# Linear attention's scan: key-value products kept in their PSUM bank for the state scans, with the first product terms placed later in the order

## The chip, the cores and the metric

The kernel runs on one NeuronCore of a Trainium2 chip, as one program. The metric is the device time of one execution, in microseconds, lower is better. Engine names in the text: PE is TensorE, DVE is VectorE, ACT is ScalarE, POOL is GpSimd.

## What is computed

The whole program is a two-layer model on x of shape 16 x 256 x 128, all float32: a linear attention block with decaying state, a mixture of experts with capacity limits, a retention block, and two layers of windowed local attention with a feed-forward part. The change lies in the first of them. Cut to what matters:

```
q, k, v = x @ Wq.T, x @ Wk.T, x @ Wv.T          # 32 heads of D = 4
q, k = rope(q), rope(k); phi = elu(.) + 1
beta = clip(sigmoid(x @ Wbeta.T + b), 0.85, 0.9995)      # M = 2 decays a head
mix = softmax(x @ Wmix.T + b)
K = K * beta + phi_k                              # (D) for each m
S = S * beta + outer(phi_k, v)                    # (D x D) for each m
num = phi_q . S ;  den = phi_q . K + 1e-6
y = sum over m of num / den * mix
z = LN(x + y @ Wout.T + bout) * g + b ;  x = x + z
```

## The kernel before, in words

Activations lie transposed, 128 features on partitions and the 4096 tokens along the free dimension, cut into 8 chunks of 512 tokens (two sequences each). `linear_attention` handles one chunk in one step c of an unrolled loop that each engine writes out in its own order; engines meet only through counting semaphores. A step works on chunk c (states and sums), on chunk c+1 (its projections, rotation and features, called "more" in the code) and on chunk c-1 (its two layer norms, called "last").

A float32 matmul over 512 tokens is two passes on PE, shown in the profile as a pair. The eight PSUM banks are fixed: 0 and 1 take projections (k, q and their swapped forms) and the centred x, 2 is shared by denominators, values, variances and the router, 3 to 6 are the "spread" banks (BV + d), 7 collects the output sum.

For each of the four d (rows of the state) of a chunk:

- `keys_spread` (L494, PE) copies feature d of phi_k to all four rows of its head, into bank 3 + d.
- `outer` (L722, DVE) multiplies that bank with the values vs and writes `U[d]` in SBUF; this counts `u_done`.
- `state` (L726, DVE), twice for each d (states i = 2d and 2d + 1, one for each decay m), scans `S[i] = beta * S + U[d]` along the tokens. It counts `s_scan`.
- `queries_spread(c, i)` (L512, PE), i = 0 to 7, spreads the query share of decay i % 2 into bank 3 + i % 4. The first four of them take over a bank that keys_spread had filled, the other four a bank that an earlier term has read.
- `term(c, i)` (L734, DVE) multiplies that bank with S[i] into a buffer T[i % 4]; `summed(c, i)` (L519, PE) multiplies it with the output matrix and adds it up in bank 7.

Around these stand `rotate` (L699, L700, DVE), which empties banks 0 and 1, `rope` (L843), `key_dot` (L831), `divide` (L838) and `weigh` (L847) on POOL, `inverse` on ACT, `queries` (L482, L483, PE), and the norms of chunk c-1: `residual` (L738), `z_variance` (L529), `z_scale` (L742), `x_add` (L747), `x_centre` (L537), `router` (L546), `x_variance` (L562), `root` on ACT and `x_scale` (L758), the last DVE instruction of a step.

The guard that decides when the first four query spreads may overwrite their bank, and the scan:

```
                    if i < 4:
                        pe.wait_ge(u_done, 4 * c + i + 1)
                    else:
                        pe.wait_ge(t_done, NS * c + i - 3)
...
                    nc.vector.tensor_tensor(U[d][:], ps[BV + d][:], vs[c % 2][:], ALU.mult).then_inc(u_done, 1)
...
                    nc.vector.tensor_tensor_scan(S[i][:], beta[i % 2][:, chunk(c)], U[i // 2][:], 0.0,
```

Of the kernel before, what the change touches and what calls it, by code (L numbers as in the profile page):

```python
# [11 lines left out]
ALU = mybir.AluOpType  # L12
# [13 lines left out]
NH0, D0, M0 = 32, 4, 2  # L26
# [32 lines left out]
def chunk(c):  # L59
    return bass.ds(c * CH, CH)  # L60
# [282 lines left out]
def linear_attention(k, w):  # L343
    nc, ps = k.nc, k.ps
    with ExitStack() as big:
# [82 lines left out]
        with ExitStack() as ctx:  # L428
            buf = lambda n: k.sb(n, [P, CH], ctx=ctx)
            ka, kb, qa, qb, ek, eq, phk, phq = map(buf, ("ka", "kb", "qa", "qb", "ek", "eq", "phk", "phq"))  # L430
            vs = [buf(f"vs{i}") for i in range(2)]
            U = [buf(f"U{d}") for d in range(D0)]
            S = [buf(f"S{i}") for i in range(2 * D0)]
            K = [buf(f"K{m}") for m in range(M0)]
            mixed = [buf(f"phq_mixed{m}") for m in range(M0)]
# [32 lines left out]
            def _(pe):  # L468
# [37 lines left out]
                def queries_spread(c, i):  # L506
                    pe.wait_ge(shared, 2 * c + i % 2 + 1)
                    if i < 4:
                        pe.wait_ge(u_done, 4 * c + i + 1)
                    else:  # L510
                        pe.wait_ge(t_done, NS * c + i - 3)
                    nc.tensor.matmul(ps[BV + i % 4][:], w["spread"][:, i // 2, :], share[i % 2][:],  # L512
                                     start=True, stop=True).then_inc(p_mm, 1)

                def summed(c, i):
                    pe.wait_ge(t_done, NS * c + i + 1)
                    if i == 0 and c > 0:
                        pe.wait_ge(z_done, c)
                    nc.tensor.matmul(ps[BO][:], wout[:], TT[i % 4][:], start=(i == 0), stop=(i == NS - 1)).then_inc(sum_mm, 1)  # L519
# [44 lines left out]
                for c in range(-1, NCH + 1):  # L564
                    last, now, more = 0 < c, 0 <= c < NCH, c + 1 < NCH
                    if more:
                        keys(c + 1)
                    if last:
                        summed(c - 1, 6)
                        summed(c - 1, 7)  # L570
                    if now:
                        keys_spread(c, 2)
                        denominator(c, 0)
                    if more:
                        keys_swapped(c + 1)
                    if now:
                        denominator(c, 1)
                        keys_spread(c, 3)
                    if more:
                        values(c + 1)  # L580
                    if now:
                        queries_spread(c, 0)
                        queries_spread(c, 1)
                    if last:
                        z_variance(c - 1)
                    if more:
                        queries(c + 1)
                    if now:
                        queries_spread(c, 2)
                        queries_spread(c, 3)  # L590
                        summed(c, 0)
                        summed(c, 1)
                        queries_spread(c, 4)
                        queries_spread(c, 5)
                        summed(c, 2)
                        summed(c, 3)
                    if last:
                        x_centre(c - 1)
                    if now:
                        queries_spread(c, 6)  # L600
                        queries_spread(c, 7)
                    if 1 < c and c - 2 < EARLY // 4:
                        router(c - 2)
                    if last:
                        x_variance(c - 1)
                    if now:
                        summed(c, 4)
                        summed(c, 5)
                    if more:
                        keys_spread(c + 1, 0)  # L610
                        keys_spread(c + 1, 1)
# [80 lines left out]
            def _(dve):  # L692
# [3 lines left out]
                def rotate(c, which):  # L696
                    mm, a, b = ((k_mm, ka, kb), (q_mm, qa, qb))[which]
                    dve.wait_ge(mm, c + 1)
                    nc.vector.tensor_tensor(a[:], ps[BK][:], cos, ALU.mult)  # L699
                    nc.vector.tensor_tensor(b[:], ps[BKS][:], sin, ALU.mult).then_inc(rot, 1)  # L700

                def features(c, which):
                    e, x1, out = ((ek, kb, phk), (eq, qb, phq))[which]
                    dve.wait_ge(exped, 2 * c + 1 + which)
                    dve.wait_ge(plus1, 2 * c + 1 + which)
                    if c > 0 and which == 0:
                        dve.wait_ge(u_mm, 4 * c)
                    if c > 0 and which == 1:
                        dve.wait_ge(kp_done, 2 * c)
                        dve.wait_ge(mixed_r, 2 * c)  # L710
                    nc.vector.scalar_tensor_tensor(out[:], e[:], 1.0, x1[:], ALU.min, ALU.max).then_inc(phi, 1)
# [7 lines left out]
                def outer(c, d):  # L719
                    dve.wait_ge(u_mm, 4 * c + d + 1)  # L720
                    dve.wait_ge(v_sb, c + 1)
                    nc.vector.tensor_tensor(U[d][:], ps[BV + d][:], vs[c % 2][:], ALU.mult).then_inc(u_done, 1)  # L722

                def state(c, i):
                    dve.wait_ge(u_done, 4 * c + i // 2 + 1)
                    nc.vector.tensor_tensor_scan(S[i][:], beta[i % 2][:, chunk(c)], U[i // 2][:], 0.0,  # L726
                                                 ALU.mult, ALU.add).then_inc(s_scan, 1)

                def term(c, i):
                    dve.wait_ge(p_mm, NS * c + i + 1)  # L730
                    dve.wait_ge(s_scan, NS * c + i + 1)
                    if NS * c + i >= 4:
                        dve.wait_ge(sum_mm, NS * c + i - 3)
                    nc.vector.tensor_tensor(TT[i % 4][:], ps[BV + i % 4][:], S[i][:], ALU.mult).then_inc(t_done, 1)  # L734
# [25 lines left out]
                for c in range(-1, NCH + 1):  # L760
# [23 lines left out]
                    if now:  # L784
                        outer(c, 2)
                        state(c, 3)
                        term(c, 0)
                        term(c, 1)
                        outer(c, 3)
                        state(c, 4)  # L790
                    if more:
                        rotate(c + 1, 1)
                        features(c + 1, 0)
                    if now:
                        state(c, 5)
                        term(c, 2)
                    if last:
                        z_scale(c - 1)
                    if now:
                        term(c, 3)  # L800
                    if last:
                        x_add(c - 1)
                    if now:
                        state(c, 6)
                        term(c, 4)
                        term(c, 5)
                        state(c, 7)
                        term(c, 6)
                    if more:
                        features(c + 1, 1)  # L810
# [1721 lines left out]
```

## Time and profile before

| what | us |
|---|---|
| median of 3 runs | 1468.37 |
| lowest, highest run | 1466.29, 1468.88 |
| span of the profiled execution | 1407.0 |
| PE busy over the span | 1211.5 (86%) |
| DVE busy | 1044.5 (74%) |
| ACT busy | 884.2 (63%) |
| POOL busy | 841.7 (60%) |
| scan stage of linear attention, about 64 to 329 | 265 |

The profiled execution has no separate time of its own; its span runs from its first to its last instruction, and what lies outside that span is the difference to the runs, 1468.37 - 1407.0 = 61.4 us. Shares over the whole span are averages over stages with different limits, and the change touches one stage only, the stretch from 64 to about 304 us in which the chunks run through, so the views that count are those cut to one step of that stretch. A row of the timeline begins with the start in us from the span's start and the time the row covers; xN is how many instructions were merged in it, and the bracket is the idle time of that engine before it with what ended it.

### The profile page before, as it was taken

The numbers are of one execution on the slowest core, as the hardware profiler recorded it, in microseconds if no ns is written. First come the engines' busy times: TensorE is split into PE (matmuls) and PEld (weight loads), VectorE is DVE, ScalarE is ACT, GpSimd is POOL, SyncE is SP. The second block draws the span as 40 slices with busy tenths as digits, with TensorE's granted clock in tenths as the row PEclk, the third lists the DMA queues.
The fourth block names the chain that finished last, engine by engine and source line by source line (L and its number), as shares of the span: only waits on it lengthen the run. The fifth ranks groups of instructions, "written<-read, shape, count | busy, mean of one in ns | idle before, by whom it ended". The sixth has DMA issues, their size and how long they took to land. (4 is left out here: it accounts for less than half of the span.)

```text
span 1407.0 us, 26525 instructions
## 1 busy us (share of the span) xinstructions
PE 1211.5 (86%) x7852; PEld 790.4 (56%) x7852; DVE 1044.5 (74%) x2575; ACT 884.2 (63%) x2302; POOL 841.7 (60%) x774
## 2 busy tenths in 40 slices
PE   6879999973777999399689999998978999999797
PEld 3333344422556888234367777774656777777465
DVE  1289999885797998456488888874648888888564
ACT  6623333332444665067489989996648898899674
POOL 0045443514771666331788888886658887788663
PEclk9899999985898999589799999999999999999999
DMA  4800000001321221410000000000000000000001
GB/s 111 288 1 0 1 0 1 1 0 58 106 93 65 71 73 56 161 35 0 23 1 3 2 0 1 0 2 1 1 23 2 2 3 1 1 0 1 1 1 60
DMA packets 35021, 43.99 MB, mean 31 GB/s; under 512 B 5620, under 2 KB 24977, under 8 KB 34912
## 3 DMA queue, kind: packets, MB, share of 16 engines
q1 hardware_dynamic: 30304, 34.27, 7.5%
q0 software_dynamic: 4608, 8.47, 1.9%
q8 instruction: 43, 0.70, 0.2%
q14 instruction: 66, 0.54, 0.1%
HBM read 22.65 MB, written 21.12 MB: 31 GB/s over the span
## 5 line engine op out<-in xcount | busy, mean ns | idle before, releaser
L2099 DVE TENSOR_TENSOR R<-bank,tab 128x1024 f32<-128x1024 f32 x128 | 156.0, 1224 | 70.2 <-ACT sq L2009 69.4
L2043 ACT ACTIVATE W<-W,nm 128x128 f32<-128x128 f32 x512 | 198.3, 393 | 0.4
L1797 POOL TENSOR_TENSOR R<-R 128x512 f32<-128x512 f32 x128 | 161.1, 1280 | 16.0 <-DVE R L2099 16.0
L2122 DVE CUSTOM_DVE_ANT_0 W<-bank,mask_q,rn 128x128 f32<-128x128 f32 x512 | 147.5, 345 | 17.4 <-PE bank L1918 12.8
L1812 POOL TENSOR_TENSOR W<-W,rden 128x512 f32<-128x512 f32 x128 | 132.5, 1040 | 40.6 <-DVE rden L2129 35.2
L1308 POOL DMA_INDIRECT expert_rows<-Yt,xin x80 | 82.6, 1032 | 67.8 <-DVE Yt L1281 49.8
L1011 POOL DMA_INDIRECT expert_slots<-tok_rows,dst x64 | 67.5, 1054 | 66.4 <-ACT tok_rows L1035 45.6
L2043 ACT ACTIVATION_READ_ACCUMULATOR W<-W,nm 128x1 f32 x512 | 98.7, 193 | 0.0
L2027 ACT ACTIVATE QK<-bank 128x512 f32<-128x512 f32 x128 | 75.1, 587 | 35.6 <-PE bank L1893 33.7
L726 DVE TENSOR_TENSOR_SCAN S<-beta,U 128x512 f32<-128x512 f32 x64 | 93.5, 1483 | 0.0
L1943 PE MATMUL bank<-PT,VA 128*64 128x128 f32 (+1 forms) x1024 | 85.8, 261 | 3.7 <-ACT PT L2051 2.8
L1918 PE MATMUL bank<-QK 64*64 64x128 f32 x2048 | 86.1, 283 | 3.3 <-DVE nm L2122 3.0
L1806 POOL TENSOR_TENSOR R<-R,rn 128x512 f32<-128x512 f32 x64 | 66.7, 1042 | 31.3 <-ACT rn L2017 27.2
L2009 ACT ACTIVATE sq<-bank 128x512 f32<-128x512 f32 x128 | 74.6, 583 | 11.2 <-PE bank L1872 10.6
L2051 ACT ACTIVATE PT<-bank 128x512 f32<-128x512 f32 x128 | 74.9, 590 | 6.6 <-PE bank L1928 6.6
L2221 POOL TENSOR_TENSOR Uf_lo<-Uf,Uf_hi 128x512 fp32r<-128x512 f32 (+1 forms) x48 | 61.1, 1285 | 26.9 <-DVE Uf_hi L2378 26.2
L2106 DVE TENSOR_REDUCE sums<-sq 128x16 f32<-128x1024 f32 x64 | 76.9, 1201 | 0.0
L1928 PE MATMUL bank<-ident,W 128*128 128x128 f32 x512 | 75.6, 273 | 0.0
L1943 PEld LDWEIGHTS bank<-PT,VA 128*64 128x64 f32 x1024 | 52.0, 137 | 40.6 <-issue 40.5
L1872 PE MATMUL bank<-wqkv_hi,hs_hi 128*128 128x512 f32 x128 | 64.1, 501 | 10.5 <-ACT QK L2027 4.0
L1928 PEld LDWEIGHTS bank<-ident,W 128*128 128x128 f32 x512 | 62.5, 140 | 15.9 <-issue 0.7
L1918 PEld LDWEIGHTS bank<-QK 64*64 64x64 f32 x2048 | 55.3, 133 | 20.9 <-issue 16.9
(350 smaller groups left out, 3481.2 us busy)
## 6 DMA issues: line engine op xcount, KB each, us to landing
expert_slots<-empty SPq DMA_DIRECT2D x8, 650.0 KB, 6.6
xin<-expert_slots SPq DMA_DIRECT2D x8, 650.0 KB, 4.0
expert_rows<-empty SPq DMA_DIRECT2D x8, 512.0 KB, 6.7
pair_rows<-expert_rows SPq DMA_DIRECT2D x16, 256.0 KB, 4.4
expert_raw<-w1e_dram SPq DMA_DIRECT2D x9, 256.0 KB, 2.9
expert_raw<-w2e_dram SPq DMA_DIRECT2D x9, 256.0 KB, 3.2
tok<-x_dram SPq DMA_DIRECT2D x8, 256.0 KB, 4.7
out_dram<-tok_out SPq DMA_DIRECT2D x8, 256.0 KB, 2.6
```

The source lines that it names most:

```text
L726: nc.vector.tensor_tensor_scan(S[i][:], beta[i % 2][:, chunk(c)], U[i // 2][:], 0.0, ALU.mult, ALU.add).then_inc(s_scan, 1)
L1308: nc.gpsimd.indirect_dma_start(k.ys[:, :], bass.IndirectOffsetOnAxis(ap=ids, axis=0), Yt[:, s % 3, t, :], None, bounds_check=2 * T - 1, oo ...
L1797: nc.gpsimd.tensor_tensor(halves[:, :, 0, :, z, :], halves[:, :, 0, :, z, :], halves[:, :, 1, :, 1 - z, :], ALU.add).then_inc(summed, 1)
L1812: nc.gpsimd.tensor_tensor(x, x, scale.to_broadcast([P, 4, P]), ALU.mult).then_inc(scaled, 1)
L1918: m = nc.tensor.matmul(ps[BS[i]][r:r + WIN, blk // 2 * P:(blk // 2 + 1) * P], QK[par][rows, b, o:o + WIN], keys, start=True, stop=True)
L1928: m = nc.tensor.transpose(ps[BT[p % 2]][:, a * P:(a + 1) * P], W[:, p % RING, a * P:(a + 1) * P], k.const["ident"][:])
L1943: m = nc.tensor.matmul(ps[BO[p % 2]][i * DH:(i + 1) * DH, cols], v[:, 2 * b + i, :], PT[:, p % 2, i * SEQ + cols.start:i * SEQ + cols.stop ...
L2027: nc.scalar.activation(QK[par][:, qk * NB:(qk + 1) * NB, t * P:(t + 1) * P], ps[BX[(t + 1) % 2]][:].rearrange("p (a b) -> p a b", a=NB), A ...
L2043: m = nc.scalar.activation(x, x, ACT.Exp, scale=-1.0, bias=nm[:, p % RING, j:j + 1], accum_out=den[:, p % RING, j:j + 1])
L2099: nc.vector.tensor_tensor(R[:, i, qk, :, :].rearrange("p c (h d) -> p c h d", d=DH), x, y.to_broadcast([P, 2, HEADS, DH]), ALU.mult).then_ ...
L2106: nc.vector.tensor_reduce(sums[:, i, :, 0:1].rearrange("p h o -> p (h o)"), sq[:].rearrange("p q (h d) -> p (q h) d", d=DH), AX.X, ALU.add ...
L2122: m = nc.vector.tensor_tensor_reduce(W[:, p % RING, j * P:(j + 1) * P], ps[BS[i]][:, cols], k.const["mask_q"][:, cols], rn[:, par, 2 * s + ...
```

## The change

It drops the four buffers U. `outer` writes its product over the same bank that it reads, and the two scans of that d read the bank. As the bank is now needed until both scans are done, the first four `queries_spread` wait for the scans. On DVE the first terms are moved behind later scans: all eight scans are issued before term 3. On PE the sums of the terms are moved to match.

```diff
-            U = [buf(f"U{d}") for d in range(D0)]
@@ queries_spread
                     if i < 4:
-                        pe.wait_ge(u_done, 4 * c + i + 1)
+                        pe.wait_ge(s_scan, NS * c + 2 * i + 2)
@@ TensorE's order
                     if now:
+                        summed(c, 0)
                         queries_spread(c, 2)
+                        summed(c, 1)
                         queries_spread(c, 3)
-                        summed(c, 0)
-                        summed(c, 1)
+                        summed(c, 2)
                         queries_spread(c, 4)
                         queries_spread(c, 5)
-                        summed(c, 2)
-                        summed(c, 3)
                     if last:
                         x_centre(c - 1)
                     if now:
                         queries_spread(c, 6)
+                        summed(c, 3)
                         queries_spread(c, 7)
@@ outer, state
-                    nc.vector.tensor_tensor(U[d][:], ps[BV + d][:], vs[c % 2][:], ALU.mult).then_inc(u_done, 1)
+                    nc.vector.tensor_tensor(ps[BV + d][:], ps[BV + d][:], vs[c % 2][:], ALU.mult).then_inc(u_done, 1)
-                    nc.vector.tensor_tensor_scan(S[i][:], beta[i % 2][:, chunk(c)], U[i // 2][:], 0.0,
+                    nc.vector.tensor_tensor_scan(S[i][:], beta[i % 2][:, chunk(c)], ps[BV + i // 2][:], 0.0,
@@ VectorE's order
                         outer(c, 2)
                         state(c, 3)
-                        term(c, 0)
-                        term(c, 1)
                         outer(c, 3)
                         state(c, 4)
                     if more:
                         rotate(c + 1, 1)
+                    if now:
+                        term(c, 0)
+                        state(c, 5)
+                    if more:
                         features(c + 1, 0)
                     if now:
-                        state(c, 5)
-                        term(c, 2)
+                        term(c, 1)
+                        state(c, 6)
                     if last:
                         z_scale(c - 1)
                     if now:
-                        term(c, 3)
+                        term(c, 2)
+                        state(c, 7)
                     if last:
                         x_add(c - 1)
                     if now:
-                        state(c, 6)
+                        term(c, 3)
                         term(c, 4)
                         term(c, 5)
-                        state(c, 7)
                         term(c, 6)
```

TensorE, a middle chunk, from the second query spread to the sixth. Before (share0 and share1 are the query shares of the two decays, T0 to T3 the term buffers, z0_sq the square of the previous chunk's z):

```order
L512 MATMUL bank4<-phq_share1,spread 128x512 [waits u_done,phq_shared]
L529 MATMUL bank2<-z0_sq,mean 128x512 [waits v_sb,z_squared]
L482 MATMUL bank0<-H,wq0 128x512 [waits rot]
L483 MATMUL bank1<-H,wq0s 128x512
L512 MATMUL bank5<-phq_share0,spread 128x512 [waits u_done,phq_shared]
L512 MATMUL bank6<-phq_share1,spread 128x512 [waits u_done,phq_shared]
L519 MATMUL bank7<-T0,wout_centred 128x512 [waits z_done,t_done]
L519 MATMUL bank7<-T1,wout_centred 128x512 [waits t_done]
L512 MATMUL bank3<-phq_share0,spread 128x512 [waits t_done,phq_shared]
L512 MATMUL bank4<-phq_share1,spread 128x512 [waits t_done,phq_shared]
```

and in the changed kernel:

```order
L511 MATMUL bank4<-phq_share1,spread 128x512 [waits s_scan,phq_shared]
L528 MATMUL bank2<-z0_sq,mean 128x512 [waits v_sb,z_squared]
L481 MATMUL bank0<-H,wq0 128x512 [waits rot]
L482 MATMUL bank1<-H,wq0s 128x512
L518 MATMUL bank7<-T0,wout_centred 128x512 [waits z_done,t_done]
L511 MATMUL bank5<-phq_share0,spread 128x512 [waits s_scan,phq_shared]
L518 MATMUL bank7<-T1,wout_centred 128x512 [waits t_done]
L511 MATMUL bank6<-phq_share1,spread 128x512 [waits s_scan,phq_shared]
L518 MATMUL bank7<-T2,wout_centred 128x512 [waits t_done]
L511 MATMUL bank3<-phq_share0,spread 128x512 [waits t_done,phq_shared]
L511 MATMUL bank4<-phq_share1,spread 128x512 [waits t_done,phq_shared]
```

The spreads into banks 4, 5 and 6 now wait for scans instead of outer products, and the sums of T0 and T1 stand ahead of the spreads into banks 5 and 6.

VectorE, a middle chunk, the end of a step from the seventh state (S6) on. Before:

```order
L726 SCALAR_TENSOR_TENSOR S6<-beta0,U3 128x512 [waits u_done]
L734 TENSOR_TENSOR T0<-bank3,S4 128x512 [waits sum_mm,s_scan,p_mm]
L734 TENSOR_TENSOR T1<-bank4,S5 128x512 [waits sum_mm,s_scan,p_mm]
L726 SCALAR_TENSOR_TENSOR S7<-beta1,U3 128x512 [waits u_done]
L734 TENSOR_TENSOR T2<-bank5,S6 128x512 [waits sum_mm,s_scan,p_mm]
L711 SCALAR_TENSOR_TENSOR phq<-eq,qb 128x512 [waits kp_done,phq_mixed,plus1,exped]
L734 TENSOR_TENSOR T3<-bank6,S7 128x512 [waits sum_mm,s_scan,p_mm]
```

and in the changed kernel:

```order
L725 SCALAR_TENSOR_TENSOR S6<-beta0,bank6 128x512 [waits u_done]
L741 SCALAR_TENSOR_TENSOR zg0<-z0,vec0,z0_rs 128x512 [waits z_rstd]
L733 TENSOR_TENSOR T2<-bank5,S2 128x512 [waits sum_mm,s_scan,p_mm]
L725 SCALAR_TENSOR_TENSOR S7<-beta1,bank6 128x512 [waits u_done]
L746 TENSOR_TENSOR XT<-XT,zg0 128x512 [waits x_biased,z_scaled]
L733 TENSOR_TENSOR T3<-bank6,S3 128x512 [waits sum_mm,s_scan,p_mm]
L733 TENSOR_TENSOR T0<-bank3,S4 128x512 [waits sum_mm,s_scan,p_mm]
L733 TENSOR_TENSOR T1<-bank4,S5 128x512 [waits sum_mm,s_scan,p_mm]
L733 TENSOR_TENSOR T2<-bank5,S6 128x512 [waits sum_mm,s_scan,p_mm]
L710 SCALAR_TENSOR_TENSOR phq<-eq,qb 128x512 [waits kp_done,phq_mixed,plus1,exped]
```

Before, two terms stand behind the last scan; now five do.

## Rows read from the trace of the kernel before

**Rows 1.** One step of the scan stage: windows view (length, busy by engine, PE clock, DMA, GB/s).

```profile
192.14:220.43 28.29, 27.70 (x69) 11.90 (x68) 26.17 (x32) 9.98 (x17) 12.84 (x9) 1.00 0.00 0
```

**Rows 2.** The same step on DVE: timeline (start, us covered, instruction, xcount, idle before).

```profile
192.14 0.69 DVE L758 TENSOR_TENSOR H<-bank,x_rs 128x512 f32<-128x512 f32 x1 [1.61 <-ACT x_rs L662]
...
197.44 3.45 DVE L726 TENSOR_TENSOR_SCAN S<-beta,U 128x512 f32<-128x512 f32 x3
...
202.57 1.69 DVE L726 TENSOR_TENSOR_SCAN S<-beta,U 128x512 f32<-128x512 f32 x1
...
205.96 1.21 DVE L726 TENSOR_TENSOR_SCAN S<-beta,U 128x512 f32<-128x512 f32 x1
207.09 0.66 DVE L699 TENSOR_TENSOR qa<-bank,rope 128x512 f32<-128x512 f32 x1
207.67 0.68 DVE L700 TENSOR_TENSOR qb<-bank,rope 128x512 f32<-128x512 f32 x1
...
208.87 2.28 DVE L726 TENSOR_TENSOR_SCAN S<-beta,U 128x512 f32<-128x512 f32 x1
...
211.66 0.74 DVE L742 SCALAR_TENSOR_TENSOR zg<-z,vec,z_rs 128x512 f32<-128x512 f32 x1
...
215.83 1.21 DVE L726 TENSOR_TENSOR_SCAN S<-beta,U 128x512 f32<-128x512 f32 x1
```

**Rows 3.** The same step on PE: timeline; x2 is one float32 matmul.

```profile
202.09 2.26 PE L512 MATMUL bank<-phq_share,spread 128*128 128x512 f32 x4
204.19 1.02 PE L529 MATMUL bank<-z_sq,mean 128*128 128x512 f32 x2
...
205.91 1.02 PE L483 MATMUL bank<-H,wq0s 128*128 128x512 f32 x2
...
214.87 1.88 PE L512 MATMUL bank<-phq_share,spread 128*128 128x512 f32 x4
216.59 0.95 PE L546 MATMUL bank<-wr,H 128*128 128x8 f32 x8
217.92 1.10 PE L562 MATMUL bank<-x_sq,mean 128*128 128x512 f32 x2 [0.38 <-ACT empty L652]
```

**Rows 4.** The same step on POOL: timeline.

```profile
208.43 1.64 POOL L843 TENSOR_TENSOR qa<-qa,qb 128x512 f32<-128x512 f32 x1 [3.10 <-DVE qb L700]
```

**Rows 5.** Groups by line: scans from SBUF and from a bank (busy us, mean ns).

```profile
L726 DVE TENSOR_TENSOR_SCAN S<-beta,U 128x512 f32<-128x512 f32 x64 | 93.5, 1483 | 0.0
...
L1638 DVE TENSOR_TENSOR_SCAN st<-dec,bank 128x512 f32<-128x512 f32 x8 | 9.8, 1219 | 7.1 <-PE bank L1519 7.1
```

**Rows 6.** The other steps' borders on DVE: timeline.

```profile
104.38 4.05 DVE L717 TENSOR_TENSOR_SCAN K<-beta,phk 128x512 f32<-128x512 f32 x2
...
133.45 0.69 DVE L758 TENSOR_TENSOR H<-bank,x_rs 128x512 f32<-128x512 f32 x1 [0.20 <-ACT x_rs L662]
...
163.84 0.69 DVE L758 TENSOR_TENSOR H<-bank,x_rs 128x512 f32<-128x512 f32 x1 [1.62 <-ACT x_rs L662]
...
277.03 0.69 DVE L758 TENSOR_TENSOR H<-bank,x_rs 128x512 f32<-128x512 f32 x1 [1.61 <-ACT x_rs L662]
...
303.18 0.69 DVE L758 TENSOR_TENSOR H<-bank,x_rs 128x512 f32<-128x512 f32 x1 [2.96 <-ACT x_rs L662]
```

**Rows 7.** PE around its longer idle stretches: timeline.

```profile
73.54 1.98 PE L494 MATMUL bank<-phk,spread 128*128 128x512 f32 x4 [1.98 <-DVE phk L711]
...
84.12 1.91 PE L478 MATMUL bank<-H,wk0s 128*128 128x512 f32 x2
...
306.70 1.12 PE L529 MATMUL bank<-z_sq,mean 128*128 128x512 f32 x2 [1.50 <-ACT z_sq L646]
310.88 2.08 PE L537 MATMUL bank<-XT,centre 128*128 128x512 f32 x2 [3.06 <-DVE XT L747]
```

**Rows 8.** PE's granted clock there: windows view (length, PE busy, clock).

```profile
309.00:310.00 1.00, 0.00 (x0) 0.50 0.00 0
...
87.00:88.00 1.00, 1.00 (x3) 0.99 0.02 8
```

## The prediction

> **What bounds the kernel now.** I read the windows view first, cut to one step of the scan stage from one x_scale to the next. It lasts 28.29 us, DVE is busy 26.17 of them and PE 27.70, at full clock [rows 1]. The reader should see that neither has room: a reordering that makes one wait for the other is paid almost in full. Second, the timeline of DVE [rows 2]. It has one wait worth naming, 1.61 us ahead of x_scale, and two scans that take 1.69 and 2.28 us where the plain one takes 1.21; the longer one runs while POOL adds qa and qb, which is itself stretched to 1.64 us [rows 4]. Third, the timeline of PE [rows 3]: pairs start 0.86 us apart (two between 204.19 and 205.91) and the bank of one is ready 1.02 us after its start. Two pairs of which one had to wait for its input take 2.10 (202.09 to 204.19); I take 0.95 for one that waits and starts at once. x_scale comes 2.51 us after x_variance starts (217.92, and the step ends at 220.43), and x_variance 1.33 us after the router's first matmul. So a step ends with PE's queue, then ACT's root, then x_scale, and the next step starts with x_scale on DVE.
>
> **The change, part by part.**
>
> *Buffers U dropped, scans read a bank.* No instruction goes. A scan of this shape from a bank takes 1219 ns in another stage; the S scans' mean of 1483 ns holds the stretched ones [rows 5]. I take 1.22 for 1.21; the bound above is 0.03 more for each scan, about 2 us over the stage, below it is nothing. Writing the product into a bank has no row on DVE; the nearest are the 0.58 us spacing of `rotate`, which reads a bank and writes SBUF [rows 2], and the 0.01 us that the bank adds to a scan. I take no change, with 0.1 us each as the upper bound (3 us in all). The Trainium skill ("VectorE: DVE Perf Modes", the section on the TRN2 errata) has a rule against the change: an instruction with a PSUM source pays 120 fixed cycles where one from SBUF pays 58. By that each scan would be 0.065 us longer and the stage some 4 us; rows 5 do not bear it out.
>
> *Scans off POOL's way.* With the product in a bank, a scan has one SBUF input. I take the two stretched scans as plain: 0.47 + 1.07 = 1.54 us of DVE time less in a step [rows 2].
>
> *The guard and the order.* This decides. I lay one middle step out anew, t = 0 at x_scale (192.14), each engine in its new order. Up to the start of S3 nothing moves: t = 10.43 [rows 2].
> - S3 ends at 11.65. The spread into bank 4 waited for an outer product and now waits for S3, so it starts at 11.7 (before, about 11.0). Behind it stand z_variance and the two `queries` matmuls: 12.65, 13.5, 14.35, and q is in its banks at 15.4.
> - DVE has done outer and S4 by 13.3, since T0 and T1 moved away, and then waits 2.1 us for q. The rotation takes 1.2 (from 15.4 to 16.6), T0 to 17.2.
> - PE is idle from about 15.2 to 17.3, since sum 0 now stands ahead of the spread into bank 5, which itself needs S5.
> - DVE goes on with S5 (18.3), phk (18.9), T1 (19.5), S6 (20.65), zg (21.3), T2 (21.9), S7 (23.05), with 1.12 a scan (three cover 3.45), 0.59 an ordinary operation and 0.66 for zg [rows 2].
> - PE does one sum and the spread into bank 5, then sum 1, and waits again from 20.6 to 23.1: the spread into bank 6 needs S7. Before, it started two pairs behind the `queries` matmul of 205.91, at t = 15.5 [rows 3], and no scan held it.
> - From 23.1 PE has its whole tail to do: spread 3, sum 2, spreads 4 and 5, x_centre, spread 6, sum 3, spread 7. That is 0.95 + 7 x 0.86 = 7.0, so the router starts at 30.1 (before, 216.59 - 192.14 = 24.45), x_variance at 31.4 and the next x_scale at 33.95. The terms behind S7 take about 3 us of DVE and follow the spreads, so they don't add.
>
> The step becomes 33.95 instead of 28.30: **5.65 us more**, although DVE has 1.54 us less work. What POOL and ACT do is hidden: their busy time is 12.84 and 9.98 us of the step [rows 1].
>
> *The other steps* [rows 6]. Step 1 runs from 104.38 to 134.06 (x_scale at 133.45 and 0.61), 29.7: +4.3. Step 2 is 30.39: +3.6. Steps 3 to 6 are (277.03 - 163.84) / 4 = 28.30 each: 4 x 5.65 = 22.6. Step 7 is 26.15 and has neither rotation nor queries; the same layout without them puts S7's end at 18.1 and x_scale at 28.7: +2.5. Step 0 has no norms of a previous chunk behind its tail; I take half a step's excess, 3 (between 0 and 5.65). The sum is 3 + 4.3 + 3.6 + 22.6 + 2.5 = **36.0 us**.
>
> *The clock.* Before, PE is at full level throughout a step. Now it has, in each step, idle stretches of 2.1 and 2.5 us with only three pairs between them. In the trace, an idle stretch of 1.98 us stayed at the upper level (73.54), but at 306.70, after 1.50 us idle, one pair and 3.06 us idle [rows 7], the clock fell to 0.50 (1.2 GHz) before 309 and stood there [rows 8]. The new pattern lies between the two, nearer to the second. At the lower level a pair covers 1.91 us instead of 1.02 [rows 7]; after such a fall at about 80 us the full level came back at 87.0 [rows 8], with PE at work since 82.3, three to five pairs. So a fall costs up to 2.5 us where it meets the tail. None of it counts 0, all eight steps 20 us; I take 6, a third, because part of each low stretch lies in the second idle one.
>
> **Sum: +42 us**, the profiled span 1407.0 going to 1449. Against the median of the runs, 1468.37, that is **1510**. The difference of 61.4 us between them stays as it is; other stages keep their code.
>
> **The rivals.** Less than 0.2% (2.9 us) is about what a measurement of this kernel can't tell from no change.
> - *DVE stays the bound (faster).* If the tail behind S7 fitted into slack of PE, only the lifted stretch would count: 8 x 1.54 = 12 us less, 1456. It decides where the router starts no later than now, 24.45 into a step, that is where S7 ends by t = 17.4. Against it, S7 can't end before all eight scans, and PE's 27.70 busy us of 28.29 leave no slack [rows 1]. The Trainium skill ("SBUF — State Buffer", section "Who interferes with whom") says that a DVE instruction with two SBUF inputs contends with GpSimd's reads and one with a single SBUF input doesn't. By that rule alone the change is a gain; rows 2 and 4 agree with the contention. Chance 0.03.
> - *Only half of the excess.* The wait for q at 13.3 may be shorter, if the spread into bank 4 and its followers start sooner than I have them, and POOL's earlier shares may pull work forward: 1.5 to 3 us a step, 15 to 25 in all, 1483 to 1493. Chance 0.06.
> - *The clock stays low.* If PE ran most of a step at 1.2 GHz, 30 pairs at 1.71 us (half the rate of 0.86) would be 51 us a step and the time about 1650. Against it, from 23.1 to 15.2 of the next step PE has some 26 us nearly without a gap, and the clock came back in less than 5 such us [rows 8]. Chance 0.03.
> - *The change does nothing to the order,* because the spreads were late anyway. Then 1468. The spread into bank 6 would have to be no earlier than S7's end in the trace, and it starts two pairs behind the matmul of 205.91, at about 207.6, while S7 starts at 215.83 [rows 2, 3]. Chance 0.02.
> - *The forecast,* +30 to +56: 0.86.
>
> **How the numbers follow.** The forecast's own spread is the step's replay (0.3 us a step, 2.5 in all), step 0 (3 each way), the bank's cost (0 to +5) and above all the clock (-6 to +14). I give 1497 to 1524. Faster by over 0.2%: 0.03; within: 0.02; slower: 0.95.
>
> **What would show it.** In the trace of the changed kernel: x_scale to x_scale about 34 us; PE idle for about 2 us ahead of the sum of T0, released by DVE's T, and for about 2.5 us ahead of the spread into bank 6, released by an S scan; DVE idle for 2 us ahead of qa; S scans at 1.22 us without stretched ones; DVE busy about 25 of 34 us; the granted clock at 0.50 for parts of some steps. I am wrong if the S scans from a bank are stretched too, if the step is under 31 us, or if PE's tail behind S7 is not what ends it.

## The result and the profile after

| | before | changed |
|---|---|---|
| median of the runs (lowest to highest), us | 1467.33 (1459.57 to 1468.88) | 1506.7 (1505.74 to 1508.83) |
| ratio, 95% interval | | 1.0284 (1.0257 to 1.0310) |
| last x_scale of the scan stage, us into the span | 318.63 | 360.57 |
| DVE busy over the span, us | 1044.5 | 1027.3 |

The change costs 39.4 us. The forecast was +42 and 1510, and the range of 1497 to 1524 holds the time. The last x_scale comes 41.9 us later (360.57 - 318.63); 0.85 us of this lies ahead of the stage's first matmul (64.11 before, 64.96 changed), the rest in the stage. The 2.5 us between 41.9 and 39.4 are less than the 9 us between the lowest and the highest run of before. Ratios here and below leave out executions more than 1.5% above the fastest of their kernel; only the kernel before beside the last three kernels has such executions, five that its median of 1478.25 includes.

First the windows view of the changed kernel, two middle steps from one x_scale to the next (length, then busy time of PE, PEld, DVE, ACT and POOL, PE clock, DMA share, GB/s):

```profile
178.68:212.80 34.12, 29.64 (x69) 12.32 (x68) 25.18 (x33) 10.11 (x17) 10.84 (x8) 0.95 0.00 1
212.80:246.92 34.12, 29.65 (x69) 12.32 (x68) 25.17 (x33) 10.12 (x17) 10.84 (x8) 0.95 0.00 0
```

Against [rows 1] DVE does 1.0 us less work in a step and waits 6.8 us more. PE's busy time has grown by 1.95 us with the same 69 instructions, since the clock is 0.95; the rest of its step, 4.48 us instead of 0.59, is idle. The timeline of PE in the changed kernel shows where it is idle (start, us covered, instruction, xcount, idle before):

```profile
224.57 1.10 PE L511 MATMUL bank<-phq_share,spread 128*128 128x512 f32 x2 [0.80 <-DVE S L725]
...
227.22 1.02 PE L482 MATMUL bank<-H,wq0s 128*128 128x512 f32 x2
230.22 1.46 PE L518 MATMUL bank<-T,wout_centred 128*128 128x512 f32 x2 [1.98 <-DVE T L733]
231.47 2.02 PE L511 MATMUL bank<-phq_share,spread 128*128 128x512 f32 x2
233.28 1.53 PE L518 MATMUL bank<-T,wout_centred 128*128 128x512 f32 x2
236.12 1.10 PE L511 MATMUL bank<-phq_share,spread 128*128 128x512 f32 x2 [1.31 <-DVE S L725]
237.06 1.02 PE L518 MATMUL bank<-T,wout_centred 128*128 128x512 f32 x2
...
243.06 0.95 PE L545 MATMUL bank<-wr,H 128*128 128x8 f32 x8
244.40 1.10 PE L561 MATMUL bank<-x_sq,mean 128*128 128x512 f32 x2 [0.38 <-ACT empty L651]
```

0.80, 1.98, 1.31 and 0.38 make up the 4.48 us but for 0.01. Nothing is idle between 236.12 and the router: these are the seven pairs behind the spread that waited for S7, and in [rows 3] no scan held that spread. The same step in the timeline of DVE of the changed kernel:

```profile
212.80 0.69 DVE L757 TENSOR_TENSOR H<-bank,x_rs 128x512 f32<-128x512 f32 x1 [2.96 <-ACT x_rs L661]
...
218.09 3.43 DVE L725 TENSOR_TENSOR_SCAN S<-beta,bank 128x512 f32<-128x512 f32 x3
...
228.28 0.69 DVE L698 TENSOR_TENSOR qa<-bank,rope 128x512 f32<-128x512 f32 x1 [2.15 <-PE bank L482]
...
234.76 1.21 DVE L725 TENSOR_TENSOR_SCAN S<-beta,bank 128x512 f32<-128x512 f32 x1
...
238.97 0.69 DVE L733 TENSOR_TENSOR T<-bank,S 128x512 f32<-128x512 f32 x1 [1.02 <-PE bank L511]
...
246.92 0.69 DVE L757 TENSOR_TENSOR H<-bank,x_rs 128x512 f32<-128x512 f32 x1 [2.96 <-ACT x_rs L661]
```

S7 is the scan of 234.76. Behind it DVE only follows PE, term by term. The scans' group on the page and POOL's row in the timeline, of the changed kernel, answer to [rows 4, 5]:

```profile
L725 DVE TENSOR_TENSOR_SCAN S<-beta,bank 128x512 f32<-128x512 f32 x64 | 75.9, 1207 | 0.0
```

```profile
229.65 1.26 POOL L844 TENSOR_TENSOR qa<-qa,qb 128x512 f32<-128x512 f32 x1 [4.63 <-DVE qb L699]
```

All S scans are plain, 1207 ns against a mean of 1483, and POOL's add takes 1.26 us instead of 1.64. The part of the change that was to help did help. It was the order and the guard that cost.

The granted clock of PE in the changed kernel (windows view, columns as above) falls right behind the wait for T0. It is at full level, then at half (1.2 GHz) for some 3.5 us, and full again:

```profile
230.00:231.00 1.00, 0.78 (x2) 0.30 (x2) 1.00 (x2) 0.05 (x1) 0.91 (x1) 0.94 0.00 0
231.00:232.00 1.00, 1.00 (x2) 0.50 (x2) 1.00 (x3) 1.00 (x2) 0.00 (x0) 0.50 0.00 0
...
234.00:235.00 1.00, 0.81 (x2) 0.00 (x0) 1.00 (x3) 0.00 (x0) 0.00 (x0) 0.85 0.00 0
```

**What the 61.4 us were.** The profile of before has a span of 1407.0 and the runs a median of 1468.37, and the prediction carried the difference as time outside the span. It isn't: the changed kernel's profiled execution has a span of 1507.0 and a time of 1508.83, so 1.8 us lie outside. The experiments ran on several chips, and before took 1411 us on one and 1465 to 1478 us on the others, each time with 1.8 to 1.9 us outside. On the slower chips the expert stage has waits that the profile of before lacks altogether (waits view of the changed kernel, 320 to 640 us; us in total, times, longest; "remote" is the view's name for what ended them):

```profile
ACT Gf L1060 <- remote: 79.3, 2, 53.8
...
DVE cols L323 <- remote: 14.3, 4, 5.5
```

The profiles of the four kernels on the 1411 us chip, one of them with the changed orders and guard, have no such wait; all the others except the first profile of before have them. So before's profile most likely came from a chip of the quicker kind, and its runs did not. This is inferred: no profile of before was taken on a slower chip. If both kernels pay this difference of some 60 us there, it cancels in the sum. Below, each kernel is compared with before on its own chip, or by its steps of the scan stage.

### The profile page after: what moved, and what is told of

It reads as the page before. It is cut to its first block and busy times, and to the rows that moved or that the text cites. A ratio compares the mean times of both kernels' runs of the same rounds, so it can differ in the third digit from the quotient of the medians.

```text
span 1507.0 us, 26525 instructions
## 1 busy us (share of the span) xinstructions
PE 1228.9 (82%) x7852; PEld 794.1 (53%) x7852; DVE 1027.3 (68%) x2575; ACT 882.6 (59%) x2302; POOL 823.4 (55%) x774
## 5 line engine op out<-in xcount | busy, mean ns | idle before, releaser
L1012 POOL DMA_INDIRECT expert_slots<-tok_rows,dst x64 | 63.1, 986 | 70.7 <-ACT tok_rows L1036 49.6
L511 PE MATMUL bank<-phq_share,spread 128*128 128x512 f32 x128 | 73.3, 668 | 18.9 <-DVE S L725 17.7
L518 PE MATMUL bank<-T,wout_centred 128*128 128x512 f32 x128 | 70.2, 654 | 13.9 <-DVE T L733 13.8
L1060 ACT ACTIVATE Gf<-bank,b1e 128x512 f32<-128x512 f32 x32 | 19.4, 690 | 100.4 <-remote 79.3
L2107 DVE TENSOR_REDUCE sums<-sq 128x16 f32<-128x1024 f32 x64 | 76.9, 1201 | 0.0
L725 DVE TENSOR_TENSOR_SCAN S<-beta,bank 128x512 f32<-128x512 f32 x64 | 75.9, 1207 | 0.0
```

What stands on the lines that cost most here:

```text
L2107: nc.vector.tensor_reduce(sums[:, i, :, 0:1].rearrange("p h o -> p (h o)"), sq[:].rearrange("p q (h d) -> p (q h) d", d=DH), AX.X, ALU.add ...
```

## Experiments

Three things changed together: the order on DVE, the order on PE, and the place of the products with the guard of the spreads. The first four kernels ran on one chip (before 1410.64).

**The kernel before once more,** to see how far its steps repeat.

> The kernel before, unchanged, for one look. It tells whether the profiled execution with its span of 1407.0 us is like the timed runs at 1467: if it is, the span comes out near 1407 again with a time near 1467; if that execution was a lucky one, the span comes out near 1465 and the extra 60 us lie in the expert stage, where the changed kernel's profile has ACT idle 79 us. The scan stage should be the same in both, with steps of 28.3 us and the last x_scale near 318.6.

Measured: 1407.22, span 1405.4, steps of 28.30, last x_scale at 318.80. The steps repeat to 0.01 us and the stage to 0.2. Both profiles of before are quick ones, so they don't yet say that steps can be compared across chips. What says it is the last step of the stage, which has the last chunk's sums and norms alone and is the same in all kernels with before's or the change's orders: 15.45 us on this chip (303.35 to 318.80 here) and 15.45 to 15.46 on the slower ones (345.12 to 360.57 in the changed kernel).

**Both orders, without banks and guard.**

```diff
-                        pe.wait_ge(s_scan, NS * c + 2 * i + 2)
+                        pe.wait_ge(u_done, 4 * c + i + 1)
...
-  nc.vector.tensor_tensor(ps[BV + d][:], ps[BV + d][:], vs[c % 2][:], ALU.mult)
+  nc.vector.tensor_tensor(U[d][:], ps[BV + d][:], vs[c % 2][:], ALU.mult)
```

> The new orders of DVE and PE, but products in the SBUF buffers U and the old guard (outer product done). Theory A (the guard and the order each cost, because sums stand ahead of spreads and five terms behind S7): steps of about 31.8 us, +22 to +24 us in all, 1489 to 1492. Rival B (only the guard costs, the order is harmless): steps of 28.3 to 28.8, 1467 to 1472. Rival C (the order is all of it): steps of 34 us, 1505 or more.

Measured: 1434.41, ratio 1.0177 (1.0159 to 1.0194); steps of 32.12, last x_scale +23.1. The timeline of PE in this kernel:

```profile
218.74 1.13 PE L519 MATMUL bank<-T,wout_centred 128*128 128x512 f32 x2 [1.98 <-DVE T L734]
...
221.74 1.13 PE L519 MATMUL bank<-T,wout_centred 128*128 128x512 f32 x2 [1.02 <-DVE T L734]
...
224.12 1.12 PE L519 MATMUL bank<-T,wout_centred 128*128 128x512 f32 x2 [0.39 <-DVE T L734]
```

PE waits for terms alone, 3.39 us. Two thirds of the step's excess (3.8 of 5.8) are there with the old guard. The changed kernel's guard waits come on top and hide some of these.

**Orders and guard, products in SBUF.** Against the changed kernel only outer and state differ:

```diff
-  nc.vector.tensor_tensor(ps[BV + d][:], ...).then_inc(u_done, 1)
+  nc.vector.tensor_tensor(U[d][:], ...).then_inc(u_done, 1)
-  nc.vector.tensor_tensor_scan(S[i][:], beta[i % 2][:, chunk(c)], ps[BV + i // 2][:], 0.0,
+  nc.vector.tensor_tensor_scan(S[i][:], beta[i % 2][:, chunk(c)], U[i // 2][:], 0.0,
```

> The change with its orders and its guard, but the products written to U in SBUF and scanned from there. Theory A: the scans meet POOL's additions again, two of them stretched, so steps are longer than the changed kernel's 34.1: 34.9 or so, 1513 to 1520. Rival D (reading and writing the bank is what costs): steps fall below 33.5 and the time below 1502.

Measured: 1467.69, ratio 1.0409 (1.0391 to 1.0426); steps of 37.6, last x_scale +58.7. This is longer than expected; the windows view of this kernel says why:

```profile
218.84:256.49 37.65, 32.29 (x69) 13.18 (x68) 26.79 (x32) 9.99 (x17) 12.47 (x8) 0.86 0.00 0
```

The clock is 0.86 instead of 0.95: the low stretches now reach the tail, as the timeline of PE in this kernel shows:

```profile
243.37 2.05 PE L512 MATMUL bank<-phq_share,spread 128*128 128x512 f32 x2 [0.93 <-DVE S L726]
245.21 1.92 PE L519 MATMUL bank<-T,wout_centred 128*128 128x512 f32 x2
...
252.64 0.95 PE L546 MATMUL bank<-wr,H 128*128 128x8 f32 x8
```

The spread behind S7 starts 24.53 us into the step, 1.2 later than in the changed kernel (23.32); that is what the stretched scans delay. From it to the router it takes 9.27 us instead of 6.94, and these 2.3 are the clock. Read together: the guard costs 5.5 us a step where the scans are stretched (32.1 to 37.6), the low clock in the tail included, and the bank takes 3.5 of them back (34.12). Without the bank's plain scans the change would have been slower still (1.0409 against 1.0284).

**The last product alone in SBUF.** Products 0 to 2 stay in banks, product 3 goes to a buffer, and spread 3 waits for u_done:

```diff
+            U = {d: buf(f"U{d}") for d in (3,)}
+            prod = lambda d: U[d] if d in U else ps[BV + d]
...
+                    if i < 4 and i in U:
+                        pe.wait_ge(u_done, 4 * c + i + 1)
+                    elif i < 4:
                         pe.wait_ge(s_scan, NS * c + 2 * i + 2)
```

> The change, but the fourth product (d = 3) goes to U in SBUF, so that the spread into bank 6 waits for the outer product and no longer for S7. Theory A (S7 ahead of PE's tail is one of two waits that end the step): steps of about 32.0, +19 to +21 us against before, 1486 to 1489. Rival E (the tail behind S7 is all of it): steps back at 28.5 to 29.5, 1470 to 1477. Rival F (that wait is hidden): steps stay at 34, 1505.

Measured: 1431.81, ratio 1.0156 (1.0136 to 1.0177); steps of 32.1 to 32.7, last x_scale +21.4. The timeline of PE in this kernel:

```profile
219.03 1.13 PE L522 MATMUL bank<-T,wout_centred 128*128 128x512 f32 x2 [1.98 <-DVE T L737]
...
222.30 1.02 PE L515 MATMUL bank<-phq_share,spread 128*128 128x512 f32 x2
223.71 1.12 PE L522 MATMUL bank<-T,wout_centred 128*128 128x512 f32 x2 [0.39 <-DVE T L737]
```

The spread of 222.30 is the one into bank 6, and it no longer waits. The edit frees the one spread that waited for S7, and half of the change's 41.9 us are gone, although all but one of the guards, the orders and the plain scans stay. The four middle steps are 32.4 us in the mean (298.49 - 168.88, over 4), 1.7 less than with the change; the rest of the 20.5 us is in the first steps and the last. It is the direct test of the prediction's main step: the wait for S7 is there and ends the changed kernel's step, but without it the step is still 4.1 us longer than before. What remains is close to what the two orders cost by themselves (32.12).

The next four ran on another chip (before 1464.97).

**The changed kernel once more.**

> The changed kernel, unchanged, beside the kernel before on one chip. On a chip whose kernel before takes about 1410 us, it should take 1410 + 39 to 42, 1449 to 1452, with a span near 1449 and no long idle stretch of ACT in the expert stage; the steps of the scan stage stay at 34.1 us. If the extra idle time of the expert stage belongs to the change, it shows here too and the time is near 1507.

Measured: 1504.17, ratio 1.0281 (1.0247 to 1.0314), steps of 34.12 and a last x_scale at 359.77. This chip is again one of the slower kind, so the time that was expected for a quick one wasn't tested.

**The changed kernel with PE kept busy.** It has two more matmuls, a repeat of spread 1, ahead of sum 0, and two into bank 3, which spread 4 overwrites later, behind sum 1.

```diff
                     if now:
+                        again(c)
                         summed(c, 0)
                         queries_spread(c, 2)
                         summed(c, 1)
+                        idle_work(c)
                         queries_spread(c, 3)
```

> The changed kernel with four matmuls a step added, whose results are thrown away or written twice alike: two in each of PE's idle stretches. They keep the granted clock at its upper level. Theory A with a small clock term: steps of 34.0 against 34.1, the first two steps 3 us shorter in all, 3 to 7 us faster than the changed kernel in all. Rival G (the falls of the clock carry a good part of the excess): steps of 32 or less, over 12 us faster. Rival H (the added matmuls get in the way): slower than the change.

Measured: 1502.7, ratio 1.0267 (1.0233 to 1.0302), last x_scale at 355.62. The time is 1.5 us below the changed kernel's, within the noise of the two and less than the 3 to 7 expected, so the clock's part is read from the stage. The windows view of one step of this kernel:

```profile
208.74:242.86 34.12, 31.83 (x77) 13.31 (x76) 25.18 (x32) 10.09 (x17) 10.84 (x8) 1.00 0.00 0
```

The clock is full, PE has 8 instructions more, and the step is still 34.12. In the middle steps the clock costs nothing, since the low stretch lies ahead of the wait for S7, which would have been longer by as much. What it costs is 4.15 us (359.77 - 355.62, one profile each), in the first steps and the last.

**DVE's order alone,** PE's order, guard and buffers as before:

```diff
                         state(c, 3)
-                        term(c, 0)
-                        term(c, 1)
                         outer(c, 3)
                         state(c, 4)
                         rotate(c + 1, 1)
+                        term(c, 0)
                         state(c, 5)
+                        features(c + 1, 0)
+                        term(c, 1)
+                        state(c, 6)
...
+                        term(c, 2)
+                        state(c, 7)
```

> Only DVE's order is changed; PE's order, the guard and the buffers U stay. Theory A (terms behind S7 hand their banks back late, so PE's tail starts late, whoever guards): steps of 31.6 us, +20 to +22. Rival I (PE's new order does it, sum 0 ahead of the second spreads): steps of 28.3 to 28.8, +0 to +3.

Measured: 1488.16, ratio 1.0160 (1.0128 to 1.0192); steps of about 32.1, last x_scale +23.8. The timeline of PE in this kernel, in a step of 31.87 us at full clock:

```profile
187.85 1.13 PE L519 MATMUL bank<-T,wout_centred 128*128 128x512 f32 x2 [0.26 <-DVE T L734]
190.87 1.12 PE L519 MATMUL bank<-T,wout_centred 128*128 128x512 f32 x2 [1.89 <-DVE T L734]
...
195.56 1.12 PE L519 MATMUL bank<-T,wout_centred 128*128 128x512 f32 x2 [0.99 <-DVE T L734]
```

With PE's old order the excess is the same as with both orders. DVE's order costs 3.8 us a step, whichever way PE is ordered. PE waits for T0 and T1, which now stand behind the rotation of q, and for T3, which now stands behind S7. What each of these moves costs by itself wasn't run.

**Products 0 and 1 in banks, old orders.** The diff is that of product 3 above, against before, with `U = {d: buf(f"U{d}") for d in (2, 3,)}`.

> The kernel before in both its orders, with only the products of d = 0 and 1 kept in their banks and scanned from there, their spreads guarded by the scans, and d = 2 and 3 in U. Theory A: S3 is no longer stretched by POOL (1.21 instead of 1.69), but the spread into bank 4 waits for S3, so steps of 28.8 us, within 3 us of before either way. Rival J (any guard on a scan costs as the whole change does): steps of 30 or more. Rival B (the bank idea is a gain wherever the order allows it): steps of 27.8.

Measured: 1462.02, ratio 0.9980 (0.9963 to 0.9997); last x_scale -1.0. Half of the scans are plain now (1201 ns x32, the others 1446), and the middle steps are still longer, 28.86 instead of 28.30. The guard on a spread early in the step costs more there than the plain scans give back, as the timeline of PE in this kernel shows:

```profile
202.20 1.10 PE L515 MATMUL bank<-phq_share,spread 128*128 128x512 f32 x2 [0.81 <-DVE S L729]
```

The gain comes from the first steps (-1.2 to the first x_scale, -1.1 in the next step) and step 7 (-0.85).

**PE's order alone** (last of the series; before 1466.51 on its chip):

```diff
+                        summed(c, 0)
                         queries_spread(c, 2)
-                        queries_spread(c, 3)
-                        summed(c, 0)
                         summed(c, 1)
+                        queries_spread(c, 3)
+                        summed(c, 2)
                         queries_spread(c, 4)
                         queries_spread(c, 5)
-                        summed(c, 2)
-                        summed(c, 3)
```

> Only PE's order is changed (sums of T0 and T1 ahead of the spreads into banks 5 and 6, sum 2 ahead of the third pair of spreads, sum 3 ahead of the last spread); DVE's order, the guard and the buffers U stay. With DVE's old order the terms T0 and T1 are ready when PE comes to them, so theory A gives steps of 29.4 us, +6 to +8 in all; together with DVE's order alone (32.0 measured) that is more than the two orders together (32.1), so they overlap. Rival I (PE's order is the main part of the order's cost): steps of 31 or more.

Measured: 1475.92, ratio 1.0061 (1.0041 to 1.0082); steps of 29.61, last x_scale at 326.83 (+8.0). With the old order on DVE, PE's order costs 1.3 us a step in one wait, for T2, whose sum now stands ahead of spreads 4 and 5:

```profile
245.47 1.12 PE L519 MATMUL bank<-T,wout_centred 128*128 128x512 f32 x2 [1.43 <-DVE T L734]
```

**Other orders.** If order is what costs, another one should win, with or without banks. Three kernels on one chip (before 1478.25) have both queues written anew. Their common core: outer products and states alternate early on DVE, the router and spreads stand further ahead on PE, sums further back. The diff, of the version with two products in banks, cut to the last part of a step on PE and the first on DVE (the conditions around the calls are left out):

```diff
                         queries_spread(c, 3)
-                        summed(c, 0)
-                        summed(c, 1)
                         queries_spread(c, 4)
+                        summed(c, 0)
+                        router(c - 2)
                         queries_spread(c, 5)
-                        summed(c, 2)
-                        summed(c, 3)
+                        queries_spread(c, 6)
                         x_centre(c - 1)
-                        queries_spread(c, 6)
-                        queries_spread(c, 7)
-                        router(c - 2)
+                        summed(c, 1)
+                        summed(c, 2)
...
+                        outer(c, 0)
                         key_state(c, 0)
+                        state(c, 0)
                         key_state(c, 1)
-                        outer(c, 0)
-                        outer(c, 1)
...
+                        rotate(c + 1, 0)
+                        outer(c, 1)
+                        state(c, 1)
+                        outer(c, 2)
+                        state(c, 2)
```

All products in banks, guard as in the change:

> The change's buffers and guard (all four products in their banks) with other orders on both engines: outer, K scans and S scans start a step, S5 to S7 follow each other ahead of the second rotation, the router moves ahead of the spread into bank 5, the keys' matmuls of the next chunk go behind the spreads, the sums 3 to 5 go to the end. Theory A (the idea of the change is sound and its order is what costs): steps near PE's own work, 27.0 to 27.5 us, 10 to 15 us faster than before. Rival K (waiting for both scans of a bank costs in any order): steps of 29 or more, slower than before.

Measured: 1463.5, ratio 0.9918 (0.9894 to 0.9943); steps of 27.14, last x_scale -13.5. The windows view of one of its steps:

```profile
182.90:210.04 27.14, 26.88 (x70) 12.20 (x69) 25.07 (x33) 9.88 (x17) 10.54 (x8) 1.00 0.00 0
```

PE is idle for 0.26 us of it, in a wait for POOL's product with K.

All products in SBUF, guard as before:

> The kernel before with its buffers U and its guard, reordered in the same spirit. Theory A: steps of 26.8 to 27.3, PE's own work, 11 to 16 us faster than before. Rival L (POOL's additions hold the scans from SBUF whatever the order): steps of 28 or more, within 4 us of before.

Measured: 1464.81, ratio 0.9917 (0.9890 to 0.9943); steps of 26.7 in the mean, last x_scale -15.1.

Products 0 and 1 in banks:

> Products of d = 0 and 1 in their banks, d = 2 and 3 in U, reordered. Theory A: steps of 26.8 to 27.3 as PE's work allows, and the first chunk a little earlier, 13 to 18 us faster than before and 1 to 3 us faster than the other two. Rival M (no difference between the three, since PE is the bound in all): equal within 1 us to the reordered kernel with U.

Measured: 1461.27, ratio 0.9895 (0.986 to 0.993); steps of 26.4 to 26.7, last x_scale -16.1. The windows view of one of its steps:

```profile
208.52:235.16 26.64, 26.64 (x69) 12.29 (x68) 25.86 (x34) 9.94 (x17) 10.07 (x8) 1.00 0.00 1
```

PE is busy for all of the 26.64 us. With the pairs at this spacing, only less work on PE would shorten this step. It is the quickest of the versions by its stage, and it beats both kernels; the three intervals overlap, so by time alone they can't be ranked. The version with products in SBUF differs from before in nothing but order and gains 15.1 us, so order alone gives such a gain. The version with all products in banks gains 13.5 under the change's own guard, so with that guard a kernel can still be faster than before. Each of the three has an order of its own, so what the banks themselves give or cost there isn't shown.

## Why the prediction was right

| step of the prediction | forecast | measured |
|---|---|---|
| q in its banks, DVE waits | t = 15.4, 2.1 us | 15.48, 2.15 us |
| PE waits for T0 | 2.1 us | 1.98 us |
| S7 ends, its spread starts | 23.05, 23.1 | 23.17, 23.32 |
| wait for S7 ahead of it | 2.5 us | 1.31 us |
| DVE's work in a step | -1.54 us | -1.0 us |
| router, x_variance, x_scale | 30.1, 31.4, 33.95 | 30.26, 31.60, 34.12 |
| middle steps, four | +22.6 us | +23.3 us |
| step 2; steps 0 and 1; step 7 | +3.6; +7.3; +2.5, without the clock | +5.3; +9.6; +3.8, with it |
| clock | +6 | +4.15 |
| scan from a bank | 1.22 us, none stretched | 1.207 us, none stretched |
| outer product into a bank | no change | 683 ns against 677 |
| the stage | +42 | +41.9 |

*The bound.* The replay by two in-order queues gave 33.95 us from the rows of before; the trace gives 34.12, with the same two waits. The end of S7 is where x_scale is decided: S7, seven pairs, the router, ACT's root. The wait ahead of the spread into bank 6 came out shorter because the pairs ahead of it ran at half clock and filled it. DVE's saving came out 0.5 us smaller because DVE waits eight times in a step instead of twice: an operation ahead of a wait covers 0.68 us, one with the next close behind it adds 0.59.

*The clock.* The prediction had the level fall around the two idle stretches, in some of the steps. It fell in each of steps 1 to 7 (a mean of 0.94 or 0.95 in each), right behind the wait for T0 in the step shown. The term was a third of its bound and measured 4.15. With the clock kept up, steps 0 and 1 are +7.05 (to 140.50), step 2 is 34.12 long, +3.7, step 7 is +2.9, and the last x_scale comes at 355.62, which is +37.0 where the layout without the clock gave 36.0. So the layout was about 1 us short over the stage and the clock term 1.9 us long; the errors have opposite signs, and that the sum is closer than its parts is luck. So is part of the clock term: its third of the bound stood for low stretches that lie partly in a wait, whereas the four middle steps pay nothing and the others all of it.

*Guard and order.* The prediction named them in one breath and did not split them. The runs do, by the middle step, from 28.30: PE's order alone 29.61, DVE's alone 32.1, both 32.12, both and the guard with stretched scans 37.6, with plain ones 34.12. The last two differ by 2.3 us of clock and 1.2 of stretched scans. The prediction argued most with the guard of the spread into bank 6; the later terms and sums weigh more: they make 3.8 of the 5.8 by themselves, and taking that guard away gave back 1.7.

*Outside the span.* Wrong, as told above: 1.8 us lie outside the span, and the rest of the 61.4 us is, as far as the runs show, a difference of chips. It did no harm, since the medians of both kernels hold it.

*The rivals.* DVE as the bound fell: it does less work in a step and only waits longer. Half the excess fell by 5.8 us a step, and with it the rival that the change does nothing to the order. A low clock for most of a step fell by 0.95. The Trainium skill's fixed cost of a PSUM source ("VectorE: DVE Perf Modes", TRN2 errata) would, by the prediction's estimate, have made a scan longer by 0.065 us; the group above has 1207 ns from a bank and that of K from SBUF in the same stage 1208 (groups by line of the changed kernel, 178.68 to 315.16):

```profile
L725 DVE TENSOR_TENSOR_SCAN S<-beta,bank 128x512 f32<-128x512 f32 x32 | 38.0, 1207 | 0.0
...
L716 DVE TENSOR_TENSOR_SCAN K<-beta,phk 128x512 f32<-128x512 f32 x8 | 9.3, 1208 | 0.0
```

The rule isn't borne out for this operation. The Trainium skill's rule that a DVE instruction with two SBUF inputs contends with GpSimd's reads ("SBUF — State Buffer", "Who interferes with whom") is borne out: both the scan (2.28 to 1.21 us) and POOL's add (1.64 to 1.26 us) lost their stretch, and with the same orders and guard but products in SBUF the mean of the S scans is 1436 ns again.

Still open: what in a chip makes the expert stage's waits, and why those of the changed kernel sum to 79.3 us in one profile and to 71.6 in another. It wasn't tried.

## What to carry to other kernels

When a change moves instructions in two in-order queues that feed each other, lay out one period anew from the rows before asking what an operation costs: find the last producer that a queue waits for, and count what stands behind it there. A buffer that is kept longer moves the guard of its next writer to a later event, and the whole rest of the writer's queue moves with it; keep an extra buffer for the last one, or order both queues so that the writer has other work until then. And 17.6 us less work on an engine (93.5 to 75.9 us of scans) is worth only what it shortens of the chain that ends the step: here 1.2 us a step by the earlier S7 and 2.3 by the clock, against 5.5 that the guard cost.

## What was not expected of the hardware

- One kernel takes 1411 us on one chip and 1465 to 1478 us on others. The last step of the scan stage is the same on both kinds to 0.01 us; as far as profiles show, the difference lies in waits in the expert stage whose releaser is "remote", up to 53.8 us long in the changed kernel.
- In the middle steps of the changed kernel the clock falls to 0.50 behind idle stretches of 0.80 and 1.98 us; in [rows 7] one of 1.98 us had not done it. Nor does the length of a stretch settle it: with both orders alone, the same wait of 1.98 us for T0 was followed by a matmul at full speed in one step (218.74, 1.13 us) and by one of 2.02 us in the next (250.86). With 0.86 as the mean clock of a step (orders and guard, products in SBUF) it doubled two pairs in the chain that ended the step.
- A product written into the bank from which it is read costs 6 ns in the middle steps (683 in the changed kernel, 677 before) and 1 ns within the kernel with products 0 and 1 in banks (680, 679); a scan of it costs nothing (1207 against 1208).
